# Rounding two batches of a decoder block beside the attention, and spreading the steps that follow

## What is computed

```python
x = x + attention(layernorm(x))                  # 32 query heads, 8 key/value heads, causal, then @ wo
q  = round_fp8(layernorm(x), blocks of 1x128)    # scale by 448/amax, to float8_e4m3 and back
w  = round_fp8(ctx, blocks of 128x128)
x = x + einsum("emk,enk->emn", q, w)             # the cross product, one batch with its own context
y = layernorm(x)
# routing: softmax(y @ Wg), top 1 of 8 experts, capacity 256 per expert
x = x + gate * expert(y) + silu(y @ sw1) * (y @ sw3) @ sw2     # the last term is the shared FFN
```

## Time and profile before

| | us |
|---|---|
| median of 3 runs (lowest, highest) | 1579.77 (1578.7, 1581.19) |
| the profiled execution, its own time | 1581.1 |
| its span, first to last instruction | 1579.3 |
| busy PE / DVE / POOL / ACT | 1453.4 / 1205.1 / 1022.9 / 959.4 |

### The profile page before, as it was taken

The page is one execution under the profiler, slowest core; times in us unless marked ns, Lnnn a source line. Parts: engine busy times, 40 slices in busy tenths (PEclk is TensorE's granted clock), DMA queues, the critical chain, the costliest instruction groups (busy, mean ns, idle before and its releaser), DMA issues.

```text
span 1579.3 us, 26942 instructions
## 1 busy us (share of the span) xinstructions
PE 1453.4 (92%) x8617; PEld 1274.5 (81%) x8617; DVE 1205.1 (76%) x2936; ACT 959.4 (61%) x2420; POOL 1022.9 (65%) x1006
## 2 busy tenths in 40 slices
PE   5899999999999999999999997758988887999997
PEld 4788888888878888888888886648888787899996
DVE  7678888887887887887887887976676755577775
ACT  4687777777676787887887886432121213556562
POOL 3787887887777888888898896732121213345555
PEclk9999999999999999999999999888999999899998
DMA  6435534333322433433443432121000003577766
GB/s 205 139 101 165 158 103 128 116 85 109 115 60 59 107 105 90 115 98 95 115 111 86 113 94 67 54 83 60 27 28 28 8 28 124 179 228 223 228 214 237
DMA packets 106812, 177.08 MB, mean 112 GB/s; under 512 B 16886, under 2 KB 38646, under 8 KB 106672
## 3 DMA queue, kind: packets, MB, share of 16 engines
q1 hardware_dynamic: 103920, 166.84, 35.8%
q0 software_dynamic: 2560, 8.25, 1.6%
q10 hardware_dynamic: 192, 0.26, 0.1%
HBM read 97.31 MB, written 31.98 MB: 82 GB/s over the span
## 4 chain that ended last, share of the span: by engine, by line
PE 67%; DVE 15%; ACT 8%; issue 4%; DMA 3%; POOL 2%; SPq 1%; DVEq 0%; ACTq 0%; POOLq 0%
PE bank L429 15%; PE bank L431 14%; PE bank L430 14%; PE bank L481 6%; PE bank L447 4%; PE bank L496 4%; PE bank L497 4%; PE bank L448 4%; ACT P L811 3%; DVE P L1110 2%; PE bank L421 1%; ACT xnx L833 1%; DVE Opair L1145 1%; ACT Otmp L817 1%; DVE work L1059 1%
## 5 line engine op out<-in xcount | busy, mean ns | idle before, releaser
L811 ACT ACTIVATE P<-P,mn 128x512 f32<-128x512 f32 (+3 forms) x512 | 284.8, 557 | 210.5 <-DVE mn L1110 206.6
L1532 POOL TENSOR_TENSOR P<-P,ri 128x128 f32<-128x128 f32 (+3 forms) x512 | 361.4, 737 | 22.4 <-DVE ri L1099 22.3
L1110 DVE CUSTOM_DVE_ANT_0 P<-bank,mask 128x512 f32<-128x512 f32 (+3 forms) x512 | 236.6, 480 | 97.2 <-PE bank L448 95.6
L1151 DVE TENSOR_TENSOR PTl<-bank,PTh 128x512 fp32r<-128x512 f32 (+1 forms) x384 | 229.8, 599 | 33.5 <-ACT PTh L823 30.9
L481 PE MATMUL bank<-ident,P 128*128 128x128 f32 x1280 | 202.6, 273 | 2.5 <-POOL P L1532 2.5
L823 ACT ACTIVATE PTh<-bank 128x512 fp32r<-128x512 f32 (+1 forms) x384 | 197.9, 516 | 6.3 <-PE bank L481 3.2
L447 PE MATMUL bank<-KT,QT 128*128 128x256 f32 (+2 forms) x512 | 188.7, 369 | 10.9 <-DVE mn L1110 10.9
L496 PE MATMUL bank<-PTh,VS 128*128 128x256 f32 (+2 forms) x512 | 163.2, 329 | 13.0 <-DVE PTl L1151 8.9
L429 PE MATMUL bank<-XT,Wh 128*128 128x512 f32 x384 | 162.8, 424 | 9.3 <-DVE XT L1081 3.5
L448 PE MATMUL bank<-KT,QT 128*128 128x256 f32 (+2 forms) x512 | 166.3, 325 | 0.0
L497 PE MATMUL bank<-PTl,VS 128*128 128x256 f32 (+2 forms) x512 | 156.9, 327 | 0.0
(11 more groups left out here) (202 smaller groups left out, 4231.9 us busy)
## 6 DMA issues: line engine op xcount, KB each, us to landing
RW<-in_wf SPq DMA_DIRECT2D x170, 256.0 KB, 3.1
QT<-qh SPq DMA_DIRECT2D x256, 64.0 KB, 2.0
QT<-ql SPq DMA_DIRECT2D x252, 64.0 KB, 2.0
Oraw<-in_wo SPq DMA_DIRECT2D x16, 512.0 KB, 5.3
KT<-KT SPq DMA_DIRECT2D x32, 256.0 KB, 3.0
xnx<-in_ctx SPq DMA_DIRECT2D x32, 256.0 KB, 3.5
Wraw<-in_wqkv SPq DMA_DIRECT2D x9, 768.0 KB, 5.0
saved<-Wh SPq DMA_DIRECT2D x7, 768.0 KB, 3.5
```

Source lines behind the costliest of these rows:

```text
L811: e.activation(pq, pq, ACT.Exp, bias=mn[:, z, qb:qb + 1], scale=-1.0, accum_out=rs[:, z, qb:qb + 1]).then_inc(a_exp, 1)
L1110: e.tensor_tensor_reduce(P[:, z, off[qb]:off[qb] + k], bank[n % 2][:, 0:k], mask[:, 512 - k:512], -0.125, BIG, ALU.add, ALU.min, mn[:, z, ...
L1151: e.tensor_tensor(pt_part(PTl, part), bank[2 + part][:, 0:128 * n].rearrange("p (m n) -> p m n", n=128), pt_part(PTh, part).bitcast(F32), ...
L1532: e.tensor_tensor(pq, pq, ri[:, z, qb:qb + 1].to_broadcast([128, n]), ALU.mult).then_inc(g_norm, 1)
```

## The change

It does these things:

1. Tiles of batches 0 and 1 are rounded as 8 further background jobs, in the order 10 contexts, 8 cross tiles, 6 contexts, and kept in DRAM too. The 24 jobs begin at h = 59, 61, 64, 66, ... 116, five steps for two. Four buffers (`YB`) take the place of two: `xnx` and two parts of `Wraw`.
2. Such a tile needs its layernorm early. ACT takes sums and squares at h = 64 to 72 (batch 0) and 73 to 81 (batch 1), DVE the reciprocal root at 74 to 77 and 83 to 86, ACT writes the normed tile (`norm_beside`) in the step before the job, DVE takes its largest values and scales (`beside_max`, `beside_scales`). SP loads the kept tile into T1 later (`load_t1`).
3. Two slots are passed in each head step from h = 117, from -44 on, one in the middle and one at the end. Batch 0 is turned, multiplied and prepared for routing in them, and the contexts of batch 1 are turned.
4. On DVE the slot in the middle of a step stands behind `masked(h, 1)` and `join` instead of ahead of them.
5. For batches 2 and 3, rounding, turning and multiplying are two slots apart instead of one, and stages from the third norm to `place` come two slots earlier. Statistics after the cross product are a stage of their own (`stats3`).
6. ACT and POOL do the slots -8 to -6 and the rest of the pieces ahead of the small tables.

```diff
+SIDE = NH - 11
...
-    for b in range(NB):
+    for i in range(TB):
+        plan(-36 + i, "context_turn", 0, i)
+        plan(-32 + 2 * i, "cross_turn", 0, i)
+        plan(-31 + 2 * i, "cross_product", 0, i)
+        plan(-30 + 2 * i, "stats3", 0, i)
+        plan(-22 + i, "norm3", 0, i)
+        plan(-20 + i, "route_turn", 0, i)
+        plan(-16 + i, "context_turn", 1, i)
+        plan(-6 + 2 * i, "cross_turn", 1, i)
+        plan(-5 + 2 * i, "cross_product", 1, i)
+        plan(-4 + 2 * i, "stats3", 1, i)
+    plan(-23, "rstd3", 0)
+    plan(-4, "logits", 0)
+    plan(-2, "choose", 0)
+    plan(2, "place", 0)
+    for b in range(1, NB):
         s = 16 * (b - 1)
         for i in range(TB):
-            plan(s - 13 + i if b else s - 3 + i // 2, "stats2", b, i)
-            plan(s + 1 + i, "cross_turn", b, i)
-            plan(s + 2 + i, "cross_product", b, i)
-            plan(s - 1 + i, "cross_round", b, i)
-            plan(s + 7 + i // 2, "norm3", b, i)
-            plan(s + 9 + i // 2, "route_turn", b, i)
-        plan(s - (7 if b else 2), "norm2", b)
-        plan(s + 6, "rstd3", b)
-        plan(s + 12, "logits", b)
-        plan(s + 14, "choose", b)
-        plan(s + (19 if b < NB - 1 else 15), "place", b)
-        s -= 10
-        for i in range(TB):
-            plan(s + 6 + i + i // 3, "context_turn", b, i)
+            if b > 1:
+                plan(s - 12 + i, "stats2", b, i)
+                plan(s - 9 + i, "context_turn", b, i)
+                plan(s - 7 + 2 * i, "cross_round", b, i)
+                plan(s - 5 + 2 * i, "cross_turn", b, i)
+                plan(s - 4 + 2 * i, "cross_product", b, i)
+                plan(s - 3 + 2 * i, "stats3", b, i)
+            plan(s + 5 + i // 2, "norm3", b, i)
+            plan(s + 7 + i // 2, "route_turn", b, i)
+        if b > 1:
+            plan(s - 8, "norm2", b)
+        plan(s + 4, "rstd3", b)
+        plan(s + 10, "logits", b)
+        plan(s + 12, "choose", b)
+        plan(s + (17 if b < NB - 1 else 14), "place", b)
...
-    return [61 + 4 * j for j in range(NCTX)]
+    return [59 + 5 * j // 2 for j in range(NCTX + 2 * TB)]
...
+        jobs = [("context", t) for t in range(10)] + [("cross", t) for t in range(2 * TB)]
+        jobs += [("context", t) for t in range(10, NCTX)]
+        job_at = {x: j for j, x in enumerate(jobs)}
+        free_wraw = Wraw[:, :, :].rearrange("p c n -> p (c n)")
+        YB = [xnx[:, 0, :], xnx[:, 1, :], free_wraw[:, 0:512], free_wraw[:, 512:1024]]
...
+            def norm_beside(j):
+                t = jobs[j][1]
+                wait_job_buffer(need, j)
+                need.wait_ge(v_nb, t // TB + 1)
+                e.activation(YB[j % 4], X[:, t, :], ACT.Identity, bias=ssum[:, 0, t:t + 1],
+                             scale=rstd[:, t:t + 1]).then_inc(a_norm, 1)
...
-                if h >= NH - 11:
-                    side_slot(h - NH - 15)
+                if h >= SIDE:
+                    side_slot(2 * (h - SIDE) - 44)
...
-                if h < TB:
-                    tile_sum(3 * TB + h)
-                elif h == TB:
-                    tile_means(slice(3 * TB, NT))
-                elif h <= 2 * TB:
-                    tile_squares(2 * TB + h - 1)
+                for b, at in ((3, 0), (0, 64), (1, 73)):
+                    if at <= h < at + TB:
+                        tile_sum(b * TB + h - at)
+                    elif h == at + TB:
+                        tile_means(b)
+                    elif at + TB < h <= at + 2 * TB:
+                        tile_squares(b * TB + h - at - TB - 1)
                 if h - 6 in begins:
...
+                if h + 1 in begins and jobs[begins[h + 1]][0] == "cross":
+                    norm_beside(begins[h + 1])
...
+                if h >= SIDE:
+                    side_slot(2 * (h - SIDE) - 43)
                 if h > NH + 2:
                     for _ in range(2):
                         split_piece(0, pieces.pop(0))
+            for s in (-8, -7, -6):
+                side_slot(s)
+                for _ in range(min(4, len(pieces))):
+                    split_piece(0, pieces.pop(0))
             need.wait_ge(d_k, 48)
             need.wait_ge(g_const, 1)
             e.activation(Gh[:, :, 0:8], Graw[:, :, :], ACT.Copy).then_inc(a_const, 1)
             e.activation(trib[:, :], tri[:, :], ACT.Copy).then_inc(a_const, 1)
-            for s in (-8, -7, -6):
-                side_slot(s)
-                for _ in range(min(4, len(pieces))):
-                    split_piece(0, pieces.pop(0))
             for x in range(NX - 1):
...
+            def beside_max(j):
+                t = jobs[j][1]
+                need.wait_ge(a_norm, t + 1)
+                chain(e.tensor_reduce(aam[:, t % TB, :], four(YB[j % 4]), AX.X, ALU.max, apply_absolute_value=True))
+
+            def beside_scales(j):
+                t = jobs[j][1]
+                after()
+                if t >= TB:
+                    need.wait_ge(a_kept, job_at["cross", t - TB] + 1)
+                scales(aam[:, t % TB, :], asc[:, t % TB, 0, :], asc[:, t % TB, 1, :], 1e-4).then_inc(v_bscale, 1)
...
+                if h - 1 in begins and jobs[begins[h - 1]][0] == "cross":
+                    beside_scales(begins[h - 1])
+                if h in begins and jobs[begins[h]][0] == "cross":
+                    beside_max(begins[h])
...
-                if h >= NH - 11:
-                    side_slot(h - NH - 15)
                 if 0 <= h < NH:
                     masked(h, 1)
                 if 0 <= h - 3 < NH:
                     join(h - 3)
+                if h >= SIDE:
+                    side_slot(2 * (h - SIDE) - 44)
...
+                for b, at in ((0, 74), (1, 83)):
+                    ts = slice(b * TB, b * TB + TB)
+                    if h == at:
+                        need.wait_ge(a_sq, 3 * TB + b * TB)
+                        need.wait_ge(a_mean, 6 + 2 * b)
+                        rstd_first(ts, 1.0 / D)
+                    elif at < h <= at + 3:
+                        rstd_next(ts)
+                    if h == at + 3:
+                        after()
+                        e.scalar_tensor_tensor(ssum[:, 0, ts], mv[:, ts, 0], -1.0, rstd[:, ts], ALU.mult,
+                                               ALU.mult).then_inc(v_nb, 1)
```

184 lines of the change are left out of this document (119 added, 65 removed).

## The result

The changed kernel takes 1631.56 us (median of 4 runs, 1624.88 to 1632.14), the kernel before 1580.48 on the same chip: a ratio of 1.0311, 95% interval 1.0297 to 1.0325. It is slower, and the prediction of 1541 us has the wrong sign. The profiled execution took 1631.2 us, its span 1629.0. All times are medians; the stages are of the profiled executions.

A forecast was written before the change was run, and what follows sets the result against it. PE was taken to bound the attention, DVE the last head steps, and waits the hand-over and FFN. 1581.1 + 16 - 20 - 10 - 25 = 1542.1, with the median 1.3 lower, gave 1541 us, range 1512 to 1570.

The forecast's parts named there:

- the third part: Attention: first and last scalings of jobs two apart share an ACT step; 3 us taken, bounds nothing and 30.
- the attention's term: Attention, h = 59 to 122: the denser jobs and added work cost +16 us, ends 0 and +45.
- Root groups: Attention: eight groups of the reciprocal root at 1.1 us of PE time each, 9 us.
- Norm, maximum and scales of eight tiles: Attention: eight scalings with maximum, priced like the root groups from below at 0.5 us each, 4 us.
- Bursts and density: Attention: scalings falling into the same ACT step, with DVE steps ahead of the next masks; 3 us, bounds nothing and 30.
- None passes 59.1: Attention, eight steps: ACT, POOL and DVE sums stay below 59.1 us, so by sums alone the cost is nothing.
- Rival 3: Attention, h = 61 to 119: the ACT, DVE and POOL round becomes the bound, 1.3 us a step, +75, whole 1600; chance 0.07.
- Rival 2: Attention: 40 of 72 small DVE steps blocked beside POOL, 1.05 us each, +42 instead of +16, whole 1567; chance 0.17.
- the last steps: Last head steps: DVE loses four roundings, 90 us for 109.8, -20 us, ends -29 and -8.
- the hand-over: Between attention and FFN: table wait goes behind the pieces, 7 us left of 17.4, -10 us, ends -14 and -2.
- The FFN: Shared FFN: waits for `place` vanish, the rounded tile's 3.9 stays, pairs 71, 74, 74; -25 us, ends -42 and -10.
- The last stretch: End of the shared FFN: the scatter comes one slot earlier and takes the 3.3 us wait for XN with it, -4 us.

The follow-up runs named there:

- e8: Changed kernel with 24 plain context jobs, without norm, maximum, scales, sums, squares and root groups of the first two batches: 1605.6 us, step 120 at 983.9.
- e16: e8 without the two exponent steps of each job on DVE, ACT and POOL keeping all their work: 1559.4 us, step 120 at 941.8.
- e2: Changed kernel with the eight batch jobs reading context tiles, without norm, maximum and scales: 1612.3 us, step 120 at 995.0.
- e17: e8 with the last scaling of a job and its store one step later: 1593.4 us, step 120 at 969.9.
- e1: Changed kernel with a job's maximum, scales and two exponent steps moved on DVE behind the step's last mask: 1611.2 us, step 120 at 997.0.
- e12: Changed kernel, last scaling a step later, cross scales' multiplications on ACT, lower bound left out, only the reciprocal on DVE: 1613.0 us, step 120 at 992.3.
- e10: Changed kernel with batch 1's first turn ahead of the weight pieces and the first rounded-tile loads one head step earlier: 1622.4 us.
- e9: Changed kernel with the FFN's roundings of batches 2 and 3, and their root, one slot earlier: 1624.2 us, FFN 264.9.
- e13: Changed kernel with roundings of batches 2 and 3 on DVE behind the low parts of their slot: 1626.7 us, FFN 266.1.
- e18: Changed kernel with last scaling a step later, the edits of e9, e10 and e13, and inverse sums behind the job's DVE operations: 1582.0 us, step 120 at 988.0.
- e7: Kernel before with six DVE operations appended, alone and beside POOL additions: exponent mask, SBUF addition and scale step took 0.22 to 0.31 us more beside POOL.

## Why the prediction was wrong

The step that failed is the third part of the attention's term: "The third part is new and has no row [...] I take 3, near the lower end". It measures 44.3 us (e8). The runs show in its place that DVE's two exponent operations of each job, waiting for ACT's scalings and held up beside POOL, delay the masks behind them: without them, 2.2 us are left (e16). The parts, by their own runs:

- Root groups, with the sums and squares that I put at nothing beside ACT: predicted 9, measured 11.1 together (e8 against e2). Near; the two were not measured apart.
- Norm, maximum and scales of eight tiles: predicted 4, measured 17.9 (e2 against the changed kernel).
- Bursts and density: predicted 3, bounds 0 and 30, measured 44.3, 14 of it from scalings that meet (e17 against e8). The upper bound was too low as well: I took 1.25 us, ACT's second scaling, for each of 24 jobs, and left out that the DVE operation waiting for a scaling is then held up beside POOL: 6.9 us once in e8, and 8.0 once in e17, where no two scalings meet. Four such hold-ups are e17's whole rest of 30 us.

The sentence "None passes 59.1, so by sums alone PE keeps its pace" was true and useless. e16 has the same sums for ACT and POOL (DVE's is lower, 46.1) and costs 2.2 us. What counted was what stands between the masks on DVE, and whether it is on time in the worst step of the pattern; that the place ahead of the masks alone makes the price is argued, and e1 speaks against it. Jobs 2.5 steps apart, on a kernel whose work repeats every four, meet every case within 20 steps; the trace of before has one phase only, job starts at 61, 65, 69, where DVE waited 4.6 us ahead of 16 exponent masks, and none took over 0.47 us. They could not bound another phase, and I took their silence for a low price.

Rival 3 named the place, and at +75 the price (+73 measured), and got a chance of 0.07 because "the sums stay at 93%". That the number fits is partly luck: its 1.3 us a step was a value chosen, not worked out. Rival 2's hold-ups are real: DVE's time beyond the shortest grew by some 30 us, where it reckoned 42 (40 times 1.05). But it counted small operations at 1.05 us each, and the long hold-ups were of the 512-column exponent masks; taking small ones away gained nothing (e12).

The other terms: the last steps gave 13.5 for 20, the hand-over 2 for 10. One SP load and ACT's turn were late, both behind other work in their queues, and e10 gives 9 us back. The hand-over's working listed the nine pieces and the turn behind them as 7 us; the pieces' loads came one by one (ACT waited 5.6 us for them), which was the condition of its poor end, -2, and -2.2 is what it gave. The FFN gave 7.7 for 25: I had kept POOL's wait of 3.9 per batch and let only `place` go. Both went, and low parts behind other work of DVE in their slot took their place, seven waits of 2.2 to 2.8 us, four of them behind roundings, which I did not look for. The last stretch gave 3.7 for a forecast of 4 by luck: the wait for XN that was to go is still there, 4.0 us after 3.3. With e9, e10 and e13 together, in e18, the three terms are -29.4 (127.2 to 97.8) and -20.6 (278.8 to 258.2), 50 us for the 55 forecast. These sizes were within reach, with an order of work that the change does not have.

Slips of the working that did not decide: PE's tenths are 9 from the third slice to the 24th; POOL was busy 80%, not 87%, from 200 to 280 us, where the rows of L1044 lie; by their own terms the poor end of the last steps is -10 (80 + 20 for 109.8), not -8, and the good end of the FFN -47 (202 + 30 for 278.8), not -42.

## What to carry to other kernels

When background work is made denser, don't add up busy shares: take the worst step of the common period (here 20 steps, as the jobs come every 2.5 and the kernel's own work every 4) and write down for each engine in order what stands ahead of the operation that the others wait for. Price a wait there by everything that queues up behind it, and if the trace shows one phase only, leave the upper bound of the others open. Here work moved off stages with idle engines gained 25 us, and beside an engine that is 99% busy it cost 73. Its share on ACT and POOL was nearly free (2.2 us in e16 for 24 jobs); the share on DVE, where the others wait, cost twice its own duration (42 us for some 20 us of work).

## What the runs showed of the hardware

DVE's TENSOR_SCALAR, SCALAR_TENSOR_TENSOR and TENSOR_TENSOR on SBUF alone took longer beside POOL even at 4 columns (a TENSOR_SCALAR 0.39 us for 0.17 in e7, a SCALAR_TENSOR_TENSOR up to 2.3 in the changed kernel). TENSOR_REDUCE and the addition that reads a PSUM bank did not (0.69 us with and without POOL in e7), nor did RECIPROCAL in the changed kernel (0.16 to 0.18 us in 72 cases). The Trainium skill (SBUF — State Buffer, SBUF: two separate sides) says that whoever starts first holds the shared ports for its whole instruction. The trace of e7 agrees: the first exponent mask beside POOL started at 1595.65 us and ended at 1596.40, 0.28 us after the POOL addition that was under way. The wait of 6.88 us through seven POOL instructions in e8 goes beyond it, and no run here shows why.

The clock fell with PE's waits too: steps 80 to 87 ran at a mean granted clock of 0.88, after 1.00 in the stretch before, and the next had 0.98. In these eight steps it stood at the lower level, 1.2 of 2.4 GHz, four times, 20.4 us in all, and each fall came during or up to 2 us after a wait of PE for the masks of 1.6 to 3.7 us.
